# Linear attention in fp16 halves, with a new order of turns, in a two-layer decoder on one core

## What is computed

```python
q_prime = jax.nn.relu(jnp.einsum('bhnd,fd->bhnf', q, Wqf))
k_prime = jax.nn.relu(jnp.einsum('bhnd,fd->bhnf', k, Wkf))
kv = jnp.einsum('bhnf,bhne->bhfe', k_prime, v)
qkv = jnp.einsum('bhmf,bhfe->bhme', q_prime, kv)
k_sum = jnp.sum(k_prime, axis=2)
qk_sum = jnp.einsum('bhmf,bhf->bhm', q_prime, k_sum)[..., None]
out = qkv / (qk_sum + 1e-08)
```

## Time and profile before

| | us |
|---|---|
| median of 3 runs | 964.4 |
| their lowest and highest | 963.85 and 969.45 |
| time of the profiled execution | 967.47 |
| its span | 965.7 |
| PE busy | 888.5 (92%) |
| DVE busy | 724.2 (75%) |
| ACT busy | 508.9 (53%) |
| POOL busy | 367.7 (38%) |
| mean granted TensorE clock (share of 2.4 GHz) | 0.969 |

### The profile page before, as it was taken

How to read it: one execution, slowest core, us unless ns; L and a number is a source line. 1 busy time by engine, 2 the same in 40 slices (tenths; PEclk the granted TensorE clock), 3 DMA queues, 4 the chain that set the end, 5 groups by cost and what they waited for, 6 DMA issues and landing times. The chain is left out here.

```text
span 965.7 us, 18389 instructions
## 1 busy us (share of the span) xinstructions
PE 888.5 (92%) x6740; PEld 662.4 (69%) x6740; DVE 724.2 (75%) x1745; ACT 508.9 (53%) x1227; POOL 367.7 (38%) x356
## 2 busy tenths in 40 slices
PE   5798999999999999999999869999987899998875
PEld 3455767777777777777777658877754688777543
DVE  5738767888778887788875453777997746779984
ACT  1435577666566665666656432354455633545555
POOL 3105455555455554455544530152231211522310
PEclk9899999999999999999999978999998998999998
DMA  9023141110111001111000000000000000000001
GB/s 278 21 54 68 31 111 34 34 23 11 33 33 33 25 8 33 33 33 31 2 11 1 1 1 1 2 1 1 1 2 1 33 12 1 1 1 1 1 1 44
DMA packets 34433, 25.21 MB, mean 26 GB/s; under 512 B 9332, under 2 KB 31436, under 8 KB 34380
## 3 DMA queue, kind: packets, MB, share of 16 engines
q1 hardware_dynamic: 34092, 24.23, 9.4%
q10 hardware_dynamic: 288, 0.26, 0.1%
HBM read 22.32 MB, written 2.17 MB: 25 GB/s over the span
## 5 line engine op out<-in xcount | busy, mean ns | idle before, releaser
L461 POOL CAST exp_hi<-exp_scores 128x1024 f16<-128x1024 f32 x64 | 67.0, 1047 | 218.2 <-ACT exp_scores L565 218.2
L74 PE MATMUL banks<-value_out_hi,xn_t_hi 128*128 128x256 f16 x512 | 140.2, 274 | 2.3 <-DVE X L830 2.3
L565 ACT ACTIVATE exp_scores<-banks,exp_bias,unscale 128x256 f32<-128x256 f32 x256 | 141.2, 560 | 2.1
L463 POOL TENSOR_TENSOR exp_lo<-exp_scores,exp_hi 128x1024 f16<-128x1024 f32 x64 | 138.4, 2162 | 5.1
L76 PE MATMUL banks<-value_out_hi,xn_t_lo 128*128 128x256 f16 x512 | 140.3, 274 | 0.0
L75 PE MATMUL banks<-value_out_lo,xn_t_hi 128*128 128x256 f16 x512 | 140.2, 274 | 0.0
L1002 PE MATMUL banks<-qk 128*128 128x256 f32 x512 | 121.4, 380 | 6.1 <-ACT exp_scores L565 6.0
L1002 PEld LDWEIGHTS banks<-qk 128*128 128x128 f32 x512 | 96.8, 190 | 26.7 <-issue 7.9
L830 DVE SCALAR_TENSOR_TENSOR X<-banks,colsum,X 128x256 f32<-128x256 f32 x256 | 106.2, 477 | 11.0 <-DVE colsum L821 9.6
L547 ACT ACTIVATE qk<-banks 128x512 f32<-128x512 f32 x128 | 75.9, 598 | 60.6 <-PE banks L76 60.6
L1218 POOL TENSOR_TENSOR rstd_stream<-rstd_stream,neg_half 128x2 f32<-128x2 f32 x40 | 29.1, 728 | 202.0 <-DVE rstd_stream L1366 164.0
(11 more groups left out here) (219 smaller groups left out, 1965.5 us busy)
## 6 DMA issues: line engine op xcount, KB each, us to landing
head_weights<-in_wqkv_d SPq DMA_DIRECT2D x32, 128.0 KB, 3.7
weight_absmax_rows<-across_partitions SPq DMA_DIRECT2D x15, 256.0 KB, 4.2
X<-in_x_d SPq DMA_DIRECT2D x4, 512.0 KB, 7.1
head_weights<-in_wqkvt_d SPq DMA_DIRECT2D x16, 128.0 KB, 3.4
head_weights<-in_w_o_d SPq DMA_DIRECT2D x16, 128.0 KB, 3.6
out<-X SPq DMA_DIRECT2D x8, 256.0 KB, 2.1
features_then_ternary<-in_c_fc_d SPq DMA_DIRECT2D x1, 1024.0 KB, 6.7
features_then_ternary<-in_c_proj_d SPq DMA_DIRECT2D x1, 1024.0 KB, 7.4
```

Of the source, the lines that this page charges most:

```text
L74: nc.tensor.matmul(out, lhs[0], rhs[0], start=first, stop=False)
L461: nc.gpsimd.tensor_copy(probh[:, s1_.par], prob[:, s1_.par]).then_inc(exph_ready, 1)
L463: nc.gpsimd.tensor_tensor(probl[:, s1_.par], prob[:, s1_.par], probh[:, s1_.par], ALU.subtract).then_inc(expl_ready, 1)
L565: last = nc.scalar.activation(prob[:, s1_.par, t, :], sc_ps[t // ST][:, t % ST, :], ACT.Exp, bias=nbias[:, t:t + 1], scale=unscale[:, s1_. ...
```

## The change

- The state is scaled and split once into an upper and a lower fp16 half (`g.kvh`, `g.kvl`, which lie where the ternary weights were prepared). For that, maxima are taken on DVE at steps 1 and 5, go through DRAM to all partitions, become scales in `linear_scales` at the end of step 9; ACT makes the upper halves at step 59, DVE the lower ones at step 60. `wq0`, `bdq` and `bq0` are loaded early instead of late.
- In `lin`, ACT now takes the ReLU of all four quarters of the features into fp16 (`lin_h0` to `lin_h3`), and DVE computes the remainder of each (`lin_l0` to `lin_l3`). `lin_o` becomes three fp16 matmuls in place of each fp32 one: 48 of 34 columns.
- The lengths in `work` are other numbers for all stages, and `LEAD` is 2.0 instead of 5.0.

```diff
-HOP, LEAD = 0.15, 5.0
+HOP, LEAD = 0.15, 2.0
...
+    LIN_MAX, KV_MAX, LIN_SCALE, KV_HI = 1, 5, 9, FIRST + ROUNDS * BODY
...
+        for dst, src in g.early_loads:
+            sp.dma_start(dst, src).then_inc(early_loaded, 16)
         load_prepared(2, 0)
...
+        sp.wait_ge(lin_max_ready, 5)
+        sp.dma_start(spread(5, P, 5), lin_max[:, :]).then_inc(lin_max_out, 16)
+        sp.wait_ge(lin_max_out, 16)
+        sp.dma_start(lin_rows[:, :, :].rearrange("p q s -> p (q s)"), gathered(5, P, 5)).then_inc(lin_max_in, 16)
         absmax_to_all(1, 4)
...
+            if known(i) and i == KV_HI:
+                act.wait_ge(lin_step, 9)
+                for n, (kv, hi, _) in enumerate(kv_parts):
+                    nc.scalar.activation(hi, kv, ACT.Copy, scale=g.lin_scale[:, 1 + n:2 + n]).then_inc(kv_halves, 1)
...
+        def linear_scales():
...
+            dve.wait_ge(lin_max_in, 16)
+            nc.vector.tensor_reduce(lin_all[:, :], lin_rows[:, :, :].rearrange("p q s -> p s q"), AX.X,
+                                    ALU.max).then_inc(lin_step, 1)
...
+            if i == LIN_MAX:
+
+                dve.wait_ge(early_loaded, 16 * len(g.early_loads))
+                for n, w in enumerate((g.wq0[:, :, :].rearrange("p k n -> p (k n)"), g.bdq[:, :], g.bq0[:, :])):
+                    nc.vector.tensor_reduce(lin_max[:, n:n + 1], w, AX.X, ALU.max,
+                                            apply_absolute_value=True).then_inc(lin_max_ready, 1)
+            if i == KV_MAX:
+                dve.wait_ge(kv_ready, NP)
+                for n, (kv, _, _) in enumerate(kv_parts):
+                    nc.vector.tensor_reduce(lin_max[:, 3 + n:4 + n], kv, AX.XY, ALU.max,
+                                            apply_absolute_value=True).then_inc(lin_max_ready, 1)
+            if i == LIN_SCALE:
+                linear_scales()
+            if i == KV_HI + 1:
+                dve.wait_ge(kv_halves, 2)
+                for n, (kv, hi, lo) in enumerate(kv_parts):
+                    nc.vector.scalar_tensor_tensor(out=lo, in0=kv, scalar=g.lin_scale[:, 1 + n:2 + n], in1=hi,
+                                                   op0=ALU.mult, op1=ALU.subtract)
...
-    work += ["lin_q PE 1.74", "lin_qt ACT .85", "lin_f0 PE .9", "lin_f1 ACT .6 lin_f0", "lin_f1 DVE .63 lin_f0",
-             "lin_f2 PE .9 lin_f1", "lin_f3 ACT .6 lin_f2", "lin_f3 DVE .63 lin_f2", "lin_o PE 3.66 lin_f3",
...
+    work += ["lin_q PE 1.83", "lin_qt ACT .74", "lin_f0 PE 1.0", "lin_h0 ACT .5 lin_f0", "lin_h1 ACT .5",
+             "lin_l0 DVE .61 lin_h0", "lin_l1 DVE .61 lin_h1", "lin_f1 PE 1.0", "lin_h2 ACT .5", "lin_h3 ACT .5",
+             "lin_l2 DVE .61 lin_h2", "lin_l3 DVE .61 lin_h3", "lin_o PE 1.5", "lin_den DVE .17", "lin_rden DVE .27",
...
-                nc.scalar.activation(qp[s][:, 2 * j:2 * j + 2, :], tiles(PA[s]), ACT.Relu).then_inc(lin_f[j], 1)
+            elif layer == "lin" and part.startswith("h"):
+                j = int(part[1:])
                 act.wait_ge(lin_f_full[j // 2], n[s])
+                nc.scalar.activation(qh[s][:, 2 * j:2 * j + 2, :], tiles((PA, PB)[j % 2][s]), ACT.Relu).then_inc(lin_fh[j], 1)
...
-                nc.vector.tensor_scalar(qp[s][:, 2 * j:2 * j + 2, :], tiles(PB[s]), 0.0, None, ALU.max).then_inc(
-                    lin_f[j], 1)
...
+                nc.vector.scalar_tensor_tensor(out=ql[s][:, 2 * j:2 * j + 2, :], in0=tiles((PA, PB)[j % 2][s]), scalar=0.0,
+                                               in1=qh[s][:, 2 * j:2 * j + 2, :], op0=ALU.max,
+                                               op1=ALU.subtract).then_inc(lin_f[j], 1)
...
-                        last = nc.tensor.matmul((PA, PB)[t][s][:, j * 34:(j + 1) * 34].unsqueeze(1),
-                                                qp[s][:, j, t * P:(t + 1) * P],
-                                                g.kv0[:, s:s + 1, j, :], start=True, stop=True)
+                        last = pair_matmuls(nc, (PA, PB)[t][s][:, j * 34:(j + 1) * 34],
+                                            [q[s][:, j, t * P:(t + 1) * P] for q in (qh, ql)],
+                                            [kv[:, s, j, :] for kv in (g.kvh, g.kvl)], True, True)
```

More of the change, by code:

```diff
@@ L1127, in streams_part @@
     lin_f_full, lin_f = [sem(f"lin_f_full{k}") for k in range(KT)], [sem(f"lin_f{j}") for j in range(4)]
+    lin_fh = [sem(f"lin_f_hi{j}") for j in range(4)]
     lin_o_full, lin_den, lin_rden, lin_o = (sem(f"lin_{k}") for k in ("o_full", "den", "rden", "o"))
@@ L1153, in norm_work @@
     def norm_work(layer, after, more):
[L1155 to L1163 removed]
+        return [f"{layer}_stats DVE .66 {after}", f"{layer}_aggr DVE .16", f"{layer}_eps DVE .08", f"{layer}_pow POOL .67",
+                f"{layer}_xn DVE .65", f"{layer}_turn PE .47"] + [f"{layer}_{w}" for w in more]
+    work = norm_work("lin", "", ["bias POOL 1.25 lin_xn", "xt ACT .49 lin_turn"])
+    work += ["lin_q PE 1.83", "lin_qt ACT .74", "lin_f0 PE 1.0", "lin_h0 ACT .5 lin_f0", "lin_h1 ACT .5",
+             "lin_l0 DVE .61 lin_h0", "lin_l1 DVE .61 lin_h1", "lin_f1 PE 1.0", "lin_h2 ACT .5", "lin_h3 ACT .5",
+             "lin_l2 DVE .61 lin_h2", "lin_l3 DVE .61 lin_h3", "lin_o PE 1.5", "lin_den DVE .17", "lin_rden DVE .27",
+             "lin_on DVE .75", "lin_ot PE .47", "lin_ote ACT .49", "lin_out PE 1.83", "lin_add DVE .6 lin_out lin_bias"]
+    work += norm_work("ffn", "lin_add", ["xt ACT .49", "lo DVE .6"])
     for place in range(2 * FFT + 3):
[L1165 removed]
+        for back, part in enumerate(("ab PE .87", "tanh ACT .29", "u DVE .33", "h DVE .39", "hi ACT .32", "lo POOL .64")):
             m = tile_at(place - back)
@@ L1171, in streams_part @@
                 work += [f"ffn_{name}{m} {length} {after}"]
[L1172 to L1175, removed]
-    work += norm_work("mem", "fat_add", ["xt ACT .85"])
-    work += ["mem_q PE 1.74", "mem_kbd DVE .68 fat_add", "mem_g PE 1.74 mem_xt", "mem_qt ACT .6 mem_q", "mem_ge ACT .6 mem_g"]
@@ L1178, in streams_part @@
-    for t in range(ST):
-        work += [f"mem{t}_{w}" for w in ("s PE 1.33" + (" mem_qt mem_kbd mem_ge" if t == 0 else ""),
-                                         "max DVE 1.17", "sub DVE 1.15", "exp ACT 1.05", "sum DVE 1.17", "rd DVE .2",
-                                         "pn POOL 2.2", "pt PE .92", "pte ACT 1.02", "o PE .75", "ote ACT .36")]
-    work += ["mem_out PE 1.74", "mem_go DVE .63", "mem_add DVE .63"]
-    work += norm_work("ter", "mem_add", ["xt ACT .6", "lo DVE .68"])
+    work += [f"ffn_out PE 3.03 ffn_lo{FFT - 1}", "ffn_add DVE .67"]
@@ new lines, in streams_part @@
+    work += norm_work("fat", "ffn_add", ["xt ACT .49", "e PE 1.74 fat_xn"])
+    work += ["fat_max DVE .61", "fat_exp ACT .9", "fat_rsum DVE .08", "fat_p DVE .52", "fat_pt PE .45 fat_p fat_xt",
+             "fat_pte ACT .49", "fat_out PE 1.83", "fat_add DVE .6"]
+    work += norm_work("mem", "fat_add", ["xt ACT .74"])
+    work += ["mem_q PE 1.8", "mem_kbd DVE .67 fat_add", "mem_g PE 1.74 mem_xt", "mem_qt ACT .49 mem_q", "mem_ge ACT .49 mem_g"]
+    for t in range(ST):
+        work += [f"mem{t}_{w}" for w in ("s PE 1.19" + (" mem_qt mem_kbd mem_ge" if t == 0 else ""),
+                                         "max DVE 1.13", "sub DVE 1.14", "exp ACT .96", "sum DVE 1.13", "rd DVE .17",
+                                         "pn POOL 1.86", "pt PE 1.02", "pte ACT .92", "o PE .58", "ote ACT .36")]
@@ L1546, in stage @@
                 features_first(PB[s], g.wq0, xt[s]).then_inc(lin_q_full, 1)
-            elif name in ("lin_f0", "lin_f2"):
-                k = int(part[1]) // 2
+            elif name in ("lin_f0", "lin_f1"):
+                k = int(part[1])
                 if k == 0:
```

80 lines of the change are left out of this document (59 added, 21 removed).

## The result

The change takes 933.39 us (median of 4 runs, 930.79 to 934.24), the kernel before 965.03 (4 runs beside it, 963.85 to 969.45): ratio 0.9647, 95% interval 0.9618 to 0.9676, 3.5% faster. On the median that stood ahead of the prediction, 964.4 us, this is about 930 us, where 943.5 was forecast and 932 was the lower end. The direction was right; the gain is 34 us, where 20.9 were forecast and the range reached to 32.4. Two executions far above all others, one of 4016 us of the kernel before and one of 1744 us of an experiment, are not counted in the ratios. The profiled execution of the change has a span of 932.4 us (its time 934.24), that of before 965.7, so there are 33.3 us to explain.

The account below looks back on a forecast made before the run. PE bounds the attention loop and `lin`, DVE part of the rest, dependencies the end. -18.9 (lin_o) - 6 (clock) + 4.0 (attention) + 0 (order) = -20.9 us, from 964.4 to 943.5 us; range 932 to 957.

Parts of the forecast that it names:

- The new order: Streams with `LEAD` 2: idle PE won at the end, overlap lost at the change of waves; 0, bounds -8 and +15.
- The clock: In the `lin` stretches, half-speed pieces behind five of eight `lin_o` mostly vanish: -6 us, bounds 0 and -7.5.
- lin_o, -18.9 us forecast: In `lin`, eight `lin_o` go from 30.5 to 11.6 us, as 48 fp16 matmuls of 30 ns each.
- The rule that I had weighed against the rows: Weight load takes stationary columns over 1.2 GHz, 107 ns for 128; 48 need 5.1 us, a loss of 10.
- Features: In `lin`, added ReLUs on ACT and remainders on DVE are hidden by other streams' PE work: cost nothing.
- The bound of 5: Features in `lin` without the cover of other streams: up to 0.6 us a sequence, 5 us.
- The attention part: Added maxima, scales and halves in the attention part cost +4.0 us in sum, bounds 0 and 6.
- The step at 9: Attention part: gathered maximum and eight tiny operations, 2.9 us, delay step 10's row maxima without slack: +2.7 us.
- The step at 5: Attention part: maxima of 2.6 us on DVE, of which 1.3 us reach PE: +1.3 us.
- The lower halves: End of the attention part: 2.6 us on DVE fall in its waits and cost nothing.
- the slower rival: Streams abreast want the same engine, up to 988 us; chance of slower kernel 0.05, of losing 10 to 20 us 0.10.
- the order pays: Rival: less overlap lost at the change of waves and both waves' ends tighten, 8 us more, 935; chance 0.17.

Follow-up runs that it names:

- the halves alone: The change with the old planned lengths and `LEAD` 5, everything else kept; 938.08 us, ratio 0.9707 to the kernel before.
- the order alone: The kernel before with `LEAD` 2 and the new lengths, features and `lin_o` still in fp32; 956.89 us, ratio 0.9918.
- the change again: The change itself, unaltered, repeated as the measure for runs beside it; 931.69 us, ratio 0.964 to the kernel before.
- the three `lin_o`: The change with each `lin_o` issued three times into the same banks, 144 narrow fp16 matmuls; 948.84 us, ratio 0.9807 to the kernel before.

## Why the prediction fell short

Two terms of the sum were sized too small, and one part of the gain has no cause shown. The new order was put at 0, by setting two effects against each other that no row priced; on the kernel with the halves it brought 5.4 us, 2.0 of them clock. The clock was put at 8.6 us (the part inside `lin_o` included) and gave 13.4 (those 2.0 among them), mainly because only the two `lin` stretches were counted and not even these in full. 3.2 us of idle time went with the halves alone, and no run says why.

**lin_o, -18.9 us forecast: right.** 30.5 us became 8 x 1.2 = 9.6, so -20.9 (2.6 of them clock, as in the forecast); 25 ns of spacing in place of 30. The rule that I had weighed against the rows (the Trainium skill, TensorE: Matmul & The Clock Gate, LDWEIGHTS) would have made this a loss; the trace of the change disagrees with it by a factor of four, 25 ns a load, matmul included.

**The clock, -6 us forecast (-8.6 with the part inside lin_o): right within `lin`, and a second kind of fall overlooked.** The trace says -13.4 in all. The 18.7 us of before, followed through the 150 stretches, are 3.1 at the start of the streams, 10.2 in five falls within the two `lin` stretches (582 to 590, 601 to 607, 609 to 617, 781 to 786, 802 to 810) and 5.3 in three others: 727 to 735, 920 to 928 and at the very end. The 10.2 are gone wholly, as they are with the halves alone; I had taken 8.6 of them. (With the order alone the loss in `lin` is larger, 13.6 us: there two pairs of fp32 `lin_o` stand back to back.) The start kept 2.4. The step that failed is that I counted only the two `lin` stretches: of the 5.3 us elsewhere 2.4 went too, by the order more than by the halves (4.7 are left with the halves alone, none with the order alone, 2.9 in the change). These falls are of another kind: ahead of the one at 728 in the kernel before, from 720 to 728, PE is busy for 5.2 of 8.0 us. The `mem` stretch of the change shows it in windows of 2 us:

```profile
694.00:696.00 2.00, 1.02 (x8) 0.78 (x8) 2.00 (x4) 1.24 (x2) 0.00 (x0) 1.00 0.00 0
696.00:698.00 2.00, 0.65 (x16) 0.38 (x16) 2.00 (x3) 1.58 (x2) 1.90 (x1) 0.88 0.03 8
698.00:700.00 2.00, 1.95 (x10) 1.62 (x12) 1.75 (x4) 0.57 (x2) 0.30 (x1) 0.50 0.00 0
```

Here the clock falls behind 4 us in which PE was busy for 1.67, and the time is lost when the work comes back. For this kind the Trainium skill (TensorE: Matmul & The Clock Gate, Part 1: The HAM clock gate) agrees with the trace, since it ties the fall to idle time of PE; for the kind behind the fp32 `lin_o`, with PE at 2.00 of 2.00 us, it does not. The denser order has less of this kind.

**Features, 0 forecast: 3 to 4 us too low.** The experiment without the remainders shows it. It takes out more than the change added to DVE and leaves ACT's part in, so the size is rough. The bound of 5 held as far as it can tell.

**The attention part, +4.0 forecast: right in the sum but for 0.2 to 1.8 us, wrong in its parts.** From the first scores to the start of the streams the kernel before takes 494.6 us, the change again 498.8 and the first profile of the change 500.4. The step at 9 is what I had worked out: number 10 of the scores comes 2.5 to 2.7 us late. The step at 5 makes the scores of step 6 0.9 us late, but those of step 7 only 0.2, so it costs 0.2 and not 1.3. The lower halves, put at nothing for 2.6 us in DVE's waits, take 4.9 and cost 1.1 at the end. In two of eight profiles of kernels with this code (the change's first one and that of the three `lin_o`; not the repetition) the next scores were another 1.8 us late. What differs is the clock: PE has waited 2.24 us ahead of number 10, in all of them (149.55 above), and in these two it then runs at 1.2 GHz for 3.4 us. The first profile, then the repetition at the same place:

```profile
152.00:154.00 2.00, 2.00 (x8) 1.33 (x7) 0.24 (x1) 2.00 (x5) 2.00 (x2) 0.50 0.08 9
```
```profile
151.00:153.00 2.00, 2.00 (x18) 1.70 (x17) 1.42 (x2) 2.00 (x5) 2.00 (x2) 1.00 0.08 9
```

So the scales at step 9 cost their own 2.5 to 2.7 us and, now and then, 1.8 more in clock. With them moved away PE no longer waits ahead of number 10, and neither cost shows in the traces of those kernels.

**The new order, 0 forecast: the failed step, beside the clock.** I set a gain of up to 13 us at the end against a loss of the same size at the change of waves, without a row for either. Measured on the halves, it gives 3.1 us of idle time (3.4 in the last 43.7 us, the 3 us of the overlap made good elsewhere) and 2.0 of clock; on the old kernel, in one execution of a scattered set, 6.4 and 2.3. In `mem` of the first wave, where the slower rival feared a loss, PE idles 6.0 us in place of 9.9. The loss was overrated because I took the whole overlap of 15 us as its price, although the overlap is worth only the idle time that it fills: four streams that start together keep PE busy for 34.3 of 36.2 us in the second `lin` without it.

Against the sum: -18.9 (lin_o) - 6 (clock) + 4 + 0 = -20.9 us forecast. By the split, measured: -18.9 of work and -13.4 of clock for the first two terms together, 7.4 more than the 24.9 forecast (2.6 in work, 1.6 in clock within `lin`, 2.4 elsewhere, 0.7 at the start); -6.3 of idle time, forecast 0, of which 3.2 come with the halves already and were not traced to a cause; +5.2 in the attention part, 1.2 more than forecast. 7.4 + 6.3 - 1.2 = 12.5, and 20.9 + 12.5 = 33.4, the 33.3 of the spans. Put by kernel, the same 12.5 us beyond the forecast are 5.4 for the order (3.1 idle, 2.0 clock, 0.3 work), 2.8 for the clock and 2.3 for the work that went with the halves, and their 3.2 of idle time, less the 1.2 of the attention part. The rival named "the order pays" (935 us, 0.17) came nearest. The lower end of the range, 932, took in its 8 us, but not its 8 us and the 4.8 by which the clock's term was short at once (930.7).

## To carry to other kernels

Where the granted clock falls on a busy PE, look at the form of the matmul: here narrow fp32 ones cost more than their own time, and splitting them into fp16 halves gave back 10 us in clock beside the 18 in matmuls. Two effects of a new order that point in opposite directions are not nothing; if no row prices either, keep both in the range together with the other terms' bounds, and look first at the stretches with idle PE, which a denser order can fill and which also bring the clock down. Work that must be done once belongs into the longest wait of its engine behind which nothing is due: moving the scales and the lower halves there gave another 4 us, 2.7 of them traced to it.

## What was not expected of the hardware

- 128x34 fp16 matmuls with 128x128 weights, each with a load of its own, start 25 ns apart.
- PE, busy for 2.00 of 2.00 us, falls to 1.2 GHz behind or within fp32 matmuls of 34 columns and not in fp16 ones of the same shape that last as long (2.4 GHz throughout).
- The lower halves on DVE, 128x2048 and 128x128 from fp32 and fp16 to fp16, take 4.8 to 4.9 us together, where the same operation on 128x512, with its fp32 input in PSUM, takes 0.68 (2.9 us for 2176 elements at that pace). What makes them slow was not tried.
